# A three-stage decoder layer: weights and context laid out transposed on the host, high parts by casting DMA, low parts on POOL

## The reference

```
x = x + attn(layernorm(x))            # w_qkv 3072x256, w_proj 256x1024, b_proj
x = x + xattn(layernorm(x), ctx)      # Wq 256x1024, Wk, Wv 128x1024, Wo 1024x256, bo
x = x + ffn(layernorm(x))             # wi 1024x256, wo 256x1024, LoRA of rank 16, top 2 of 8 experts
attn:  q, k, v, dots, softmax, out and projection each clipped to +-8 and cut to 12 fraction bits
xattn: softmax(q k^T / 8) v, then Wo + bo
ffn:   sum_k top_v[k] * relu(h wi^T + (h A_k^T) B_k^T) wo^T
```

## Time and profile before

| | |
|---|---|
| median of 3 runs | 730.09 us (729.47 to 730.7) |
| span of the profiled execution | 730.2 us (no other time of it is given) |
| PE, DVE, ACT, POOL busy | 92%, 75%, 57%, 37% of the span |
| granted PE clock, mean | 0.995 |
| HBM read, written | 16.16 MB, 2.10 MB |

### The profile page before, as it was taken

The page is one execution under the profiler, slowest core; times in us unless marked ns, Lnnn a source line. Parts: engine busy times, 40 slices in busy tenths (PEclk is TensorE's granted clock), DMA queues, the critical chain, the costliest instruction groups (busy, mean ns, idle before and its releaser), DMA issues.

```text
span 730.2 us, 15676 instructions
## 1 busy us (share of the span) xinstructions
PE 672.8 (92%) x5186; PEld 551.7 (76%) x5186; DVE 550.0 (75%) x1142; ACT 413.7 (57%) x1443; POOL 272.6 (37%) x610
## 2 busy tenths in 40 slices
PE   5998879989998899878989999999999889999997
PEld 4777768777886788766777877787788777888986
DVE  5879887887888789757767776677667668787775
ACT  4677756767776777764455455445544563433432
POOL 1166754454445534535354344234333532010110
PEclk9999999999999999999999999999999999999999
DMA  9135100000000000050000000000000000000000
GB/s 312 49 111 150 60 30 1 1 1 1 0 0 0 0 0 0 0 153 1 1 2 16 1 1 1 14 0 0 0 0 0 0 1 1 2 30 0 29 29 29
DMA packets 17002, 18.75 MB, mean 26 GB/s; under 512 B 2851, under 2 KB 15427, under 8 KB 16963
## 3 DMA queue, kind: packets, MB, share of 16 engines
q1 hardware_dynamic: 15330, 15.11, 6.4%
q0 software_dynamic: 1632, 3.15, 1.5%
HBM read 16.16 MB, written 2.10 MB: 25 GB/s over the span
## 4 chain that ended last, share of the span: by engine, by line
PE 35%; POOL 7%; DVE 6%; ACT 3%; issue 3%; DVEq 0%; POOLq 0%; ACTq 0%
PE bank L405 9%; PE bank L407 8%; PE bank L406 8%; POOL p_f L363 6%; PE bank L583 3%; ACT e_sb L889 2%; PE bank L595 2%; PE bank L607 1%; DVE mx L1164 1%; PE bank L729 1%; PE bank L741 1%; DVE bn_st L966 1%; DVE oT_lo L1206 1%; POOL p_int L316 0%; DVE v_sb L1137 0%
## 5 line engine op out<-in xcount | busy, mean ns | idle before, releaser
L363 POOL TENSOR_SCALAR p_f<-e_sb,rsum 128x128 f32<-128x128 f32 x256 | 95.6, 398 | 156.7 <-DVE rsum L1199 156.7
L316 POOL TENSOR_SCALAR p_int<-e_sb,rsc 128x128 int16<-128x128 f32 x256 | 116.2, 475 | 6.3 <-issue 5.7
L889 ACT ACTIVATE e_sb<-bank,neg_max 128x128 f32<-128x128 f32 x256 | 90.1, 380 | 12.1 <-DVE neg_max L1168 11.9
L804 ACT ACTIVATE sgn<-bank 128x512 bf16<-128x512 f32 x96 | 57.2, 598 | 57.6 <-PE bank L407 57.6
L819 ACT ACTIVATE e_sb<-si 128x128 f32<-128x128 int16 x256 | 75.1, 303 | 0.0
L1021 DVE SCALAR_TENSOR_TENSOR ri<-sgn,bank 128x512 int16<-128x512 bf16 x96 | 62.5, 677 | 7.3 <-ACT sgn L804 6.5
L875 ACT COPY q_sb<-bank 128x512 f32<-128x512 f32 x32 | 18.8, 587 | 84.5 <-PE bank L407 84.5
L311 POOL TENSOR_TENSOR rsc<-rsum,growth 128x8 f32<-128x8 f32 x32 | 6.7, 209 | 156.0 <-DVE rsum L1047 156.0
L889 ACT ACTIVATION_READ_ACCUMULATOR e_sb<-bank,neg_max 128x1 f32 x256 | 55.9, 218 | 0.0
L405 PE MATMUL bank<-xnT_hi,wqkvT_lo 128*128 128x512 f32 x128 | 53.6, 419 | 2.2 <-DVE ri L1021 1.3
L1175 DVE COPY aT_sb<-bank 128x512 f32<-128x512 f32 x64 | 41.2, 685 | 12.7 <-PE bank L583 12.5
(11 more groups left out here) (162 smaller groups left out, 2039.5 us busy)
## 6 DMA issues: line engine op xcount, KB each, us to landing
x_sb<-in_x SPq DMA_DIRECT2D x4, 512.0 KB, 10.3
wqkv_raw<-in_L_attn_w_qkv SPq DMA_DIRECT2D x2, 1024.0 KB, 10.2
out<-x_sb SPq DMA_DIRECT2D x8, 256.0 KB, 2.2
wqkv_raw<-in_L_attn_w_qkv SPq DMA_DIRECT2D x2, 512.0 KB, 5.1
wp_raw<-in_L_attn_w_proj SPq DMA_DIRECT2D x1, 1024.0 KB, 12.3
raw_b<-in_L_xattn_Wq SPq DMA_DIRECT2D x2, 512.0 KB, 3.3
wq_hi<-in_L_xattn_Wq POOLq DMA_DIRECT2D x2, 512.0 KB, 4.1
wo_hi<-in_L_xattn_Wo POOLq DMA_DIRECT2D x2, 512.0 KB, 8.4
```

What stands on the lines that cost most here:

```text
L316: i = nc.gpsimd.tensor_scalar(p_int[:, t, :], e_sb[:, t, :], rsc[:, t:t + 1], -0.5, ALU.mult, ALU.add)
L363: i = nc.gpsimd.tensor_scalar(p_f[:, t, :], e_sb[:, t, :], rsum[:, t:t + 1], 0.0, ALU.mult, ALU.add)
L804: nc.scalar.activation(sgn[:, m % 2, :], proj_ps[m % 2][:, :], ACT.Sign).then_inc(a_sgn, 1)
L889: last = nc.scalar.activation(e_sb[:, t, :], s_ps[hh][:, (t % 4) * P:(t % 4 + 1) * P], ACT.Exp, bias=neg_max[:, t:t + 1], scale=DH ** -0.5 ...
```

## The change

**Host.** w_qkv, w_proj, wi and wo are given to the kernel transposed and cut so that one partition's part of a slice lies in one piece; Wq, Wk, Wv and Wo become one array wB; the context and both LoRA factors are transposed.

**High parts.** POOL issues DMAs that cast fp32 to fp32r from memory straight into the high tiles: eight slices of w_q and w_k (one for each slot), two halves of w_v, w_proj, wB, wi and wo. ACT issues the first three raw loads, SP the others. Each raw load goes to the place of the low tile, and POOL subtracts in place (`make_low`). DVE does this for the first slice of q and k. The scale 4096 moves from the weights to 1/std: `inv_std` has one more multiplication for A.

**Waits.** PE waits on `w_lo`, the count of POOL's low parts: 1 before the v blocks of slot 0, 2 at slot 1, 3 at slot 2, 4 before its v blocks, 5 at slot 3, 7 before its project_out, 8 to 11 at slots 4 to 7.

**wB** is loaded behind the other weights; its six low parts move into the loop over groups 1 to 3 of A, in slots 3 and 6.

**B and C.** The context comes transposed, ACT and DVE split it from SBUF. POOL makes the FFN low parts and both parts of the LoRA factors in the first group of B, between the slots. `c_weights` is gone on PE, ACT and DVE.

```diff
@@ SP, ACT: loads
-            sp.dma_start(wqkv_raw[:, 0:4, :], rows[:, 0:4, :]).then_inc(ld_wq, 16)
-            sp.dma_start(x_sb[:, 0:GB, :], x[0:GB].rearrange("b p d -> p b d")).then_inc(ld_x0, 16)
...
+            load_x(0)
+            for s in range(2, NP):
+                sp.dma_start(wqk_raw[:, s, :, :, :], wqk[:, s, :, :, :]).then_inc(ld_qk[s], 16)
+                if s == 2:
+                    sp.dma_start(wv_raw[:, 1, :, :], wv[:, 1, :, :]).then_inc(ld_v[1], 16)
+                if s == 3:
+                    sp.dma_start(wp_raw[:, :, :], wp).then_inc(ld_wp, 16)
...
+            for s in range(2):
+                nc.scalar.dma_start(wqk_raw[:, s, :, :, :], wqk[:, s, :, :, :]).then_inc(ld_qk[s], 16)
+                if s == 0:
+                    nc.scalar.dma_start(wv_raw[:, 0, :, :], wv[:, 0, :, :]).then_inc(ld_v[0], 16)
@@ POOL, stage A
+    V_LOW = (1, 4)
+    QK_LOW = (0, 2, 3, 5, 8, 9, 10, 11)
+    WP_LOW = (6, 7)
...
+            def make_low(n):
+                raw, hi, lo, raw_in, hi_in = low_part(n)
+                pool.wait_ge(raw_in, 16)
+                pool.wait_ge(hi_in, 16)
+                nc.gpsimd.tensor_tensor(lo, raw, hi.bitcast(F32), ALU.subtract).then_inc(w_lo, 1)
+
+            for n in range(3):
+                load_high(n)
...
+                if not first and s in (3, 6):
+                    chunk = 2 * (g - 1) + (s - 3) // 3
+                    raw, hi, lo = (w[:, bass.ds(chunk, 1), :].rearrange("p a e -> p (a e)") for w in (wB_raw, wB_hi, wB_lo))
+                    nc.gpsimd.tensor_tensor(lo, raw, hi.bitcast(F32), ALU.subtract).then_inc(wB_done, 1)
+
+            inv_std(0, scaled=True)
+            make_low(1)
+            make_low(2)
             nc.gpsimd.sem_inc(a_x, 2)
 
             for s in range(NP):
                 a_slot(0, s, first=True)
-                if s == 2:
-                    pool.wait_ge(w_lo, len(PREP))
-                    for src, hi, lo in B_CHUNKS:
-                        nc.gpsimd.dma_start(hi, src).then_inc(ld_bhi, 16)
...
+                for n in ((4, 5), (6, 7, 8), (9, 10, 11), (), (), (), (), ())[s]:
+                    load_high(n)
+                for n in ((3,), (4, 5), (6, 7), (8,), (9,), (10,), (11,), ())[s]:
+                    make_low(n)
                 if s == 3:
...
+                    nc.gpsimd.dma_start(wB_hi[:, :, :], wB).then_inc(lh_wB, 16)
@@ POOL, first group of B
+                if s in (4, 6):
...
+                    nc.gpsimd.tensor_tensor(wd_lo[:, half, :], wd_raw[:, half, :], wd_hi[:, half, :].bitcast(F32),
+                                            ALU.subtract).then_inc(cw_lo, 1)
...
+                if s == 7:
+                    pool.wait_ge(ld_lb, 16 * 6)
...
+                    for k, lbT in enumerate((lb1T, lb2T)):
+                        pool.wait_ge(g_lb, 2 + 3 * k)
+                        nc.gpsimd.tensor_scalar(raw_b[0:96, :], lb_raw[:, :], lora_sign[:, k:k + 1], 0.0, ALU.mult,
                                                 ALU.add).then_inc(g_lb, 1)
-                        nc.gpsimd.tensor_copy(lb2[:, :, j, 1, :], lb_raw[:, :, 1, :]).then_inc(g_lb, 1)
+                        pool.wait_ge(g_lb, 3 + 3 * k)
+                        nc.gpsimd.tensor_copy(lbT[:, :], raw_b[0:96, :]).then_inc(g_lb, 1)
+                        pool.wait_ge(g_lb, 4 + 3 * k)
+                        nc.gpsimd.tensor_tensor(lbT[64:96, :], raw_b[64:96, :], lbT[64:96, :].bitcast(F32),
+                                                ALU.subtract).then_inc(g_lb, 1)
@@ PE
+                if first and s > 0:
+                    wait(pe, w_lo, QK_LOW[s])
...
+                if first and s == 3:
+                    wait(pe, w_lo, WP_LOW[1])
                 if not (first and s < 3):
-                    project_out(n - 3, (s - 3) % NP, a_olo, a_pj, (wpT_hi, wpT_lo), (a_z, 2 * g))
+                    project_out(n - 3, (s - 3) % NP, a_olo, a_pj, (wp_hi, wp_lo), (a_z, 2 * g))
...
-            normed_T(0, lambda: wait(pe, w_lo, 4))
-            a_weights_T(PREP_PARTS[1])
-            pe.wait_ge(w_lo, 8)
+            normed_T(0, lambda: None)
+            pe.wait_ge(w0_lo, 1)
...
-                if s == 0:
-                    pe.wait_ge(g_lb, 10)
-                    pe.wait_ge(b_e, NP * G)
-                c_weights(C_PARTS[s])
@@ DVE
             norm_moments()
+            raw, hi, lo, raw_in, hi_in = low_part(0)
+            dve.wait_ge(raw_in, 16)
+            dve.wait_ge(hi_in, 16)
+            V.tensor_tensor(lo, raw, hi.bitcast(F32), ALU.subtract).then_inc(w0_lo, 1)
             norm_apply(0, 0, (ln_T, 0))
```

More of the change, by code:

```diff
@@ L526, in a_slot @@
                     a_attend(n - 2, p, BLOCKS * gg + (block_index(1) + 4 if p < 4 else block_index(3) + 4))
+                if first and s in (0, 2):
+                    wait(pe, w_lo, V_LOW[s // 2])
                 if s < 4:
@@ L616, in b_slot @@
                 lag2 = not (first and s < 2) and not (drain and s >= 2)
-                if s == 0 and not drain:
-                    wait(pe, ld_ctx, 16 * (g + 1))
-                    wait(pe, ln_lo, 2 * (G + g) + 1)
-                    for b in range(GB):
-                        last = pe.transpose(one_ps[:, b * P:(b + 1) * P], ctx_sb[:, b, :], ident[:, :])
-                    last.then_inc(b_cT, 1)
                 def transposes():
@@ L1122, in _ @@
             xnT_low(0)
-            a_weights_low(PREP_PARTS[1])
             for s in range(NP):
```

430 lines of the change are left out of this document (185 added, 245 removed).

## The result

The changed kernel takes **755.41 us** (median of four runs, 752.91 to 756.21), the kernel before 730.05 us on the same chip. The ratio is 1.0341, with a 95% interval from 1.0323 to 1.0359: 25 us slower. I had forecast 734.6 in a range of 726.0 to 741.0. The direction was right, and the size was wrong by 21 us. The profiled execution, the longest of the four, has a span of 754.4 us against 730.2 before.

What follows compares the result with a forecast made beforehand. Time was taken as PE work (busy 672.8 of 730.2 us) or holes in it, mostly waits for POOL's softmax weights. Eleven terms summed to +4.5 on 730.1, giving 734.6 us, range 726.0 to 741.0.

Steps and rivals of the forecast that it cites:

- term 4: Stage A, first project_out: PE waits for POOL's seventh low part, the second of wp; +6.3 us (4 to 8).
- term 9: Stage B, slot 4: wd_lo ahead of the residual rows on POOL delays p_f; +0.8 us (0 to 1.5).
- term 7: Stage A, groups 1 to 3: six wB low parts behind p_int may block DVE; +0.9 us (0 to 3).
- 5: Stage A, behind the hole at the first project_out: PE clock lowered after idling; +1.7 us (0 to 2).
- 6: Seam of A group 0 to 1: Wo loads and low parts leave group 0; -5.0 us (-4 to -5.2).
- 10: End of B group 0: LoRA operations on POOL delay p_f; +3.9 us for the hole, +1.0 for the clock.
- 11: Seam B to C: weight transposes and copies go, the first up-projection comes sooner; -4.1 us (-3.3 to -6).
- Term 1: Start to first projection: x lands at 7.5, POOL's low part delays xn, projection at 18.4; +0.5 us (-3 to +3.5).
- Term 2: Start: without weight transposes as warm-up, first projections run at half rate; +1.7 us (0.5 to 2.2).
- A: Rival: POOL makes the seventh low part before PE reaches project_out, terms 4 and 5 vanish; 726.6 us, chance 0.20.
- B: Rival: start is short of DMA, x lands at 10 or later; 740 us, chance 0.14.
- C: Rival: gains and losses cancel, shorter LoRA operations and no clock loss in one hole; 730 us, chance 0.13.

Runs made afterwards that it cites:

- e1_qk_early: The changed kernel with low parts 9, 10 and 11 (wqk slices for slots 5, 6, 7) made one slot earlier on POOL; 740.01 us, ratio 1.0122.
- e12_fill: The changed kernel with 36 dummy fp32 transposes on PE ahead of each wait for wqk_lo in slots 5, 6 and 7; 750.61 us, ratio 1.0277.
- e4_no_ffn_low: e1_qk_early without POOL's four wi_lo and wd_lo operations; a casting DMA fills those arrays with other values; 733.14 us, ratio 1.0033.
- e8_ffn_dve: e1_qk_early with the four wi_lo and wd_lo operations made by DVE at the end of the same slots; 739.77 us, ratio 1.0127.
- e7_warm: e6_start plus 28 dummy fp32 transposes on PE ahead of xn; 729.61 us, ratio 0.9993.
- e6_start: e3_wp_early with lb2T made behind B's last p_f, and DVE normalising x ahead of the first slice's low part; 730.76 us, ratio 0.9997.
- e9_x_late: e7_warm with DVE waiting in slot 1 only for group 1's x, loaded ahead of wp; bias and other groups' waits in slot 4; 728.91 us.
- e3_wp_early: e1_qk_early with low parts 3 to 7 made in slots 0 and 1, PE's first project_out waiting only for the needed w_proj half; 734.75 us.

## Why the prediction was wrong

**The step that failed is in term 4, in its last sentence: "Nothing gives it back: slot 3 to 4 is not waiting for POOL."** It is true of the one slot that it names, behind low 8 (7.0 us, 7.1 before), and I went no further: the waits behind lows 9, 10 and 11 have no term, which puts them at nothing. They stand in my own list of the change. What I should have asked of each: where in POOL's order is this operation, what is ahead of it, and what does *that* wait for? Ahead of them is p_int, and the row of rsc already shows POOL standing 4.84 us for DVE. I priced POOL operations by their length and by their place behind the wait that I had in view, never by the wait ahead of them. What the runs showed in its place is a ring through POOL that makes three slots 14 to 15 us long: 16.2 us by the markers, 16.0 by e1_qk_early, of which 4.7 is clock (e12_fill).

**The second miss is the price of term 9 and an operation without a term.** I priced wd_lo at 0.8 for one place, and wi_lo nowhere. The four cost 4.7 us together, 1.2 each (e4_no_ffn_low by the markers). In term 7 I had put six such operations in the loop of A at +0.9 with a worry about DVE, and there they cost nothing (0.0). DVE is held up there too: 1.75 us for two clips at 157.51 and 1.68 for q_sb at 183.94, which take 0.50 and 0.41 alone. But no wait of PE follows. Why DVE has this room in A and not in B I did not test. The same operation is free in one stage and half on the path in the other; e8_ffn_dve shows that in B it doesn't matter which of the two engines does it.

**Right**, by the markers: terms 4 and 5 together (8.0 for 9.0), 6 (-5.0 for -4.3; the -0.7 for slot 5 lay in the ring, and shows in e1_qk_early, where slot 5 takes 8.4 for 9.1), 8 (-1.1 for -0.7), 10 (4.9 for 4.4, but divided otherwise: 2.80 of idle and 1.6 behind it, with matmuls at half rate, where I had 3.9 and 1.0; I had TENSOR_SCALAR and cast at 1.3 and they are 1.12 and 1.03) and 11 (-4.1 for -4.1). The seam before and after, as it answers to the earlier trace rows:

```profile
597.16 1.04 PE L583 MATMUL bank<-ident,p_f 128*128 128x128 f32 x8
...
625.56 1.57 PE L609 MATMUL bank<-ident,p_f 128*128 128x128 f32 x8 [3.68 <-POOL p_f L372]
...
633.61 0.40 PE L450 MATMUL bank<-xnT_hi,wi_lo 128*128 128x512 f32 x1
```

From the transposes to the first up-projection pass 11.97 us before (to 609.13) and 8.05 after: the hole of 3.7 us that I forecast is there, and so is what goes behind it.

**That term 4 met the wait to the tenth, 6.3, was luck.** Its mechanism is right, its parts are not. I read the row at 49.81 as the first matmul of project_out. It is the seventh; the first starts at 49.02:

```profile
49.02 0.36 PE L405 MATMUL bank<-wpT_hi,oT_lo 128*128 128x256 f32 x1
```

So 0.4 us were free and not 1.2. In the changed kernel the pow ends at 48.14 and PE is ready for project_out at 48.49 (54.79 less its 6.30 of wait). Each is 0.5 us sooner than before and not 2, and POOL has fallen behind PE by under 0.1 us where I had +0.5. The second low part ends 6.6 us after the pow where I had 7.0. The errors cancel.

**Term 1 was wrong, inside its range.** I had the first projection at 18.4, +0.5; it came at 16.54, -1.4. x landed at 5.99, nearly at the old 5.84 and not at 7.5, and no POOL operation was in the way of xn, because POOL itself waited 3.72 us for the cast half of w_v. In its stead DVE stood 3.17 us for the casting DMA of the first slice. **Term 2** was right: the first matmuls start 0.43 us apart, and e7_warm takes that away: from the first projection to the first scores pass 6.7 us there and 8.5 in the changed kernel, a difference of 1.75 where I had 1.7. Together terms 1 to 3 are -1.1 for +0.1. e6_start, e7_warm and e9_x_late say that gains there hardly reach the end (0.1, 0.3 and 0.9 us by the ratios). Part of the reason is in the traces: DVE stands 1.75 us for x in e7_warm, POOL 3.26 for w_v in e9_x_late. The high parts are read a second time, 22.71 MB in all instead of 16.16. I treated the start as a chain of engines, and it is also one of loads.

**The rivals.** A was out: POOL was not in time. B named a real danger, late loads, but x landed at 5.99 and not at 10, and the start came out 1.1 us shorter. C fell with the miss; its price was also wrong by its own terms, as 0.9 for shorter operations and 1.7 for one clock loss make 2.6 and not 3.5 to 5. The real case, a ring through POOL, is the sort that my list lacked: a transfer of order, not of work. My range was built from the errors of the terms that I had; it had no room for one that I had not.

## What to carry to other kernels

Work that is put on an engine with much idle time can only be free if it stands *ahead* of what that engine waits for. For every wait that a change adds, write down the instruction ahead of the releasing one on its engine and follow it back; if it comes back to the waiting engine's last slot, the pipeline is now a ring and the slot is as long as the sum. Here three operations of 1.26 us cost 16 us in one order and nothing in another.

That is needed and not enough: idle time of POOL is not independent of DVE's. The low parts of w_proj stood ahead in e3_wp_early and held a DVE operation of 0.41 us for 4.59, and in the first group of B it made no difference which of the two engines did the work.
